# Attention plus FP4 feed-forward on one core: pairing two steps of the middle batches on TensorE

## The reference

```python
x = x + attention(layernorm(x), ctx, ctx)     # ctx: 1601 rows, 16 heads of 16 features
x = x + ffn(layernorm(x))

attn = softmax(einsum('bhqd,bhkd->bhqk', q, k) * scale)
out  = einsum('bhqk,bhkd->bhqd', attn, v)
h    = silu(fp4_linear(x, w_gate)) * fp4_linear(x, w_up)   # blocks of 16 rounded to FP4
y    = fp4_linear(h, w_down)
```

## Time and profile before

| what | value |
|---|---|
| timed runs | 1724.98 us median of 3 (1724.56 to 1728.42) |
| the profiled execution | 1726.32 us, span 1724.5 us |
| TensorE busy | 1653.4 us, 96% of the span |
| VectorE / ScalarE busy | 1427.4 us (83%) / 1132.4 us (66%) |
| mean granted TensorE clock | 0.991 |

### The profile page before, as it was taken

How to read it: one execution, slowest core, us unless ns; L and a number is a source line. 1 busy time by engine, 2 the same in 40 slices (tenths; PEclk the granted TensorE clock), 3 DMA queues, 4 the chain that set the end, 5 groups by cost and what they waited for, 6 DMA issues and landing times.

```text
span 1724.5 us, 27130 instructions
## 1 busy us (share of the span) xinstructions
PE 1653.4 (96%) x9496; PEld 666.1 (39%) x9496; DVE 1427.4 (83%) x2078; ACT 1132.4 (66%) x2295; POOL 553.3 (32%) x667
## 2 busy tenths in 40 slices
PE   6899899999999999999999999999999999989978
PEld 4332234333433344333443334333443334323345
DVE  5878988988798978898889887898879887898447
ACT  3377677766777667776677667776677766666731
POOL 5238520732025320443107321263303431013303
PEclk9899999999999999999999999999999999999989
DMA  6745332431235332142323323254222323200000
GB/s 166 158 81 136 70 70 45 97 98 36 57 59 118 74 63 55 49 116 48 78 45 77 105 43 60 45 120 86 52 53 60 81 48 67 44 8 10 13 22 13
DMA packets 106771, 117.53 MB, mean 68 GB/s; under 512 B 23236, under 2 KB 88140, under 8 KB 106636
## 3 DMA queue, kind: packets, MB, share of 16 engines
q1 hardware_dynamic: 101808, 111.62, 30.7%
q10 hardware_dynamic: 4828, 4.18, 1.0%
HBM read 76.78 MB, written 30.16 MB: 62 GB/s over the span
## 4 chain that ended last, share of the span: by engine, by line
PE 82%; DVE 11%; ACT 4%; issue 2%; DMA 1%; POOL 0%; ACTq 0%; SPq 0%; DVEq 0%
PE pvb L871 21%; PE st L837 20%; PE mx L856 10%; PE misc L758 7%; DVE cmx L1120 5%; PE misc L720 5%; PE misc L713 4%; PE misc L779 3%; ACT prob L1042 2%; PE misc L771 2%; PE misc L699 2%; PE misc L767 1%; PE misc L799 1%; PE misc L808 1%; DVE ht L1149 1%
## 5 line engine op out<-in xcount | busy, mean ns | idle before, releaser
L1042 ACT ACTIVATE prob<-st 128x512 f32<-128x512 f32 (+1 forms) x1591 | 867.6, 599 | 374.7 <-PE st L837 371.2
L1120 DVE TENSOR_REDUCE cmx<-mx 128x2 f32<-128x1024 f32 x768 | 904.9, 1219 | 150.5 <-PE mx L856 145.4
L837 PE MATMUL st<-qstack,kstack 112*128 112x512 bf16 (+1 forms) x1591 | 496.9, 384 | 8.5 <-ACT prob L1042 2.4
L871 PE MATMUL pvb<-prob,vv 128*32 128x512 f32 (+1 forms) x3328 | 444.2, 606 | 0.6 <-ACT prob L1042 0.6
L837 PEld LDWEIGHTS st<-qstack,kstack 112*128 112x128 bf16 (+1 forms) x1591 | 128.1, 98 | 463.4 <-issue 236.4
L856 PE MATMUL mx<-kstack,qstack 48*128 48x512 bf16 (+1 forms) x2048 | 256.8, 336 | 18.4 <-DVE cmx L1120 18.0
L1385 POOL TENSOR_TENSOR ht<-ht,rh 128x352 f32<-128x352 f32 (+1 forms) x78 | 56.9, 751 | 418.1 <-DVE rh L1096 418.1
L758 PE MATMUL misc<-wguT,rowsT 128*128 128x352 f32 x456 | 153.7, 458 | 0.0
L1377 POOL TENSOR_TENSOR ht<-ht,mt 128x352 f32<-128x352 f32 (+1 forms) x136 | 120.8, 911 | 69.5 <-DVE mt L1283 60.1
L856 PEld LDWEIGHTS mx<-kstack,qstack 48*128 48x128 bf16 x2048 | 59.8, 94 | 199.7 <-issue 138.0
L1391 POOL TENSOR_TENSOR cin<-cin 128x400 f32<-128x400 f32 (+1 forms) x60 | 55.7, 928 | 250.6 <-ACT cin L967 250.6
(11 more groups left out here) (192 smaller groups left out, 1558.5 us busy)
## 6 DMA issues: line engine op xcount, KB each, us to landing
kstack<-scr_k SPq DMA_DIRECT2D x378, 100.1 KB, 4.4
scr_k<-cin SPq DMA_DIRECT2D x48, 300.0 KB, 4.1
qstack<-scr_q SPq DMA_DIRECT2D x372, 32.0 KB, 1.9
cin<-ctx_in SPq DMA_DIRECT2D x16, 512.0 KB, 5.4
scr_q<-qp SPq DMA_DIRECT2D x16, 384.0 KB, 4.3
scr_k<-cin SPq DMA_DIRECT2D x16, 300.8 KB, 4.8
xn<-x SPq DMA_DIRECT2D x8, 512.0 KB, 3.9
cin<-ctx_in SPq DMA_DIRECT2D x16, 256.0 KB, 5.6
```

What stands on the lines that cost most here:

```text
L837: mm(score_bank(it, n, h)[0:KROWS[kt], :], kstack[:, hd, KOFF[kt]:KOFF[kt] + KROWS[kt]], qstack[:, hd, :], start=True, stop=True).then_inc ...
L871: last = mm(pvb[2 * D * h:2 * D * (h + 1), :], vv[0:w, kt, (HG * g + h) // 2, D * (h % 2):D * (h % 2 + 2)], prob[0:w, n % 2, h, :], start= ...
L1042: activate(prob[0:KROWS[kt], n % 2, 2 * pair + h, :], score_bank(it, n, 2 * pair + h)[0:KROWS[kt], :], ACT.Exp, scale=SCALE).then_inc(exp_ ...
L1120: v.tensor_reduce(cmx[:, g % 2, h0:h0 + 2, at:at + 1], products, op=ALU.max, axis=AX.X).then_inc(max_free, 1)
```

## The change

In "loop" iterations two steps are taken together, an even step n-1 and the odd step n. `maxima_with` puts no M in the even step; the odd step does M of n-1 after its scores and M of n at its end. `weighted_behind` (all batches with attention) puts both W into the odd step: those of n-2 and n-1. VectorE's extras of the even step follow the first M, those of the odd step the second. Since W comes later, `prob` has three buffers; room for it comes from `qp` (now in `ht`), `qx` (now in `x1` or `rowsT`) and `hqT` (now in `xa`), with three new waits that guard these places. Jobs that came at even steps from the side lists move to odd steps, and some down and gate jobs trade places.

```diff
-    10: ([("k", 1, "early")], [("nm", 1, "att")]),
-    11: ([("q", 0, "early")], []),
+    10: ([("k", 1, "early")], []),
+    11: ([("q", 0, "early")], [("nm", 1, "att")]),
...
+def weighted_behind(n):
+    if n in (1, 2 * NKT, 2 * NKT + 1):
+        return [n - 1]
+    return [n - 2, n - 1] if n % 2 and n > 1 else []
...
+def maxima_with(kind, n):
+    if kind != "loop":
+        return [n], []
+    return ([n - 1], [n]) if n % 2 else ([], [])
...
-        prob = sb("prob", [128, 2, HG, S])
+        prob = sb("prob", [128, 3, HG, S])
...
-                    products = maxima(it, n)
+                    products, behind = ([job for m in steps for job in maxima(it, m)] for steps in maxima_with(it.kind, n))
...
-                    if n and has_att:
-                        weighted(n - 1, "att")
-                    elif n == 0 and has_late:
+                    for m in weighted_behind(n) if has_att else []:
+                        weighted(m, "att")
+                    if n == 0 and has_late:
                         weighted(STEPS - 1, "late")
-                    for job in products[2:]:
+                    for job in products[2:] + behind:
                         pair_products(job)
...
-                        need(act, pv_done, it.count("att", STEPS, n - 1))
+                        need(act, pv_done, it.count("att", STEPS, n - 2))
...
-                    todo = maxima(it, n)
-                    for job in todo:
-                        maximum(job)
+                    before, behind = maxima_with(it.kind, n)
+                    for m in before:
+                        for job in maxima(it, m):
+                            maximum(job)
```

More of the change, by code:

```diff
@@ L94 @@
     20: ([("gate", 0, "late"), ("bob", 0, "once")], []),
-    21: ([("gate", 1, "late")], [("nm", 2, "att")]),
-    22: ([("up", 0, "late"), ("wT", 0, "once")], [("xqT", 1, "late")]),
-    23: ([("up", 1, "late"), ("wT", 1, "once")], []),
+    21: ([("gate", 1, "late")], []),
+    22: ([("up", 0, "late"), ("wT", 0, "once")], []),
+    23: ([("up", 1, "late"), ("wT", 1, "once")], [("nm", 2, "att")]),
     24: ([("gate", 2, "late")], []),
-    25: ([("gate", 3, "late"), ("wT", 2, "once")], []),
+    25: ([("gate", 3, "late"), ("wT", 2, "once")], [("xqT", 1, "late")]),
     26: ([("up", 2, "late"), ("wT", 3, "once")], []),
     27: ([("up", 3, "late")], [("hqT", 0, "late")]),
[L102 to L113, removed]
+    28: ([("gate", 4, "late")], []),
+    29: ([("gate", 5, "late")], [("hqT", 1, "late")]),
+    30: ([("down0", 0, "late")], []),
+    31: ([("down", 0, "late"), ("wT", 4, "once")], []),
+    32: ([("up", 4, "late"), ("wT", 5, "once")], []),
+    33: ([("up", 5, "late")], [("hqT", 2, "late")]),
+    34: ([("gate", 6, "late")], []),
+    35: ([("gate", 7, "late"), ("wT", 6, "once")], [("nm", 3, "att"), ("hqT", 3, "late")]),
+    36: ([("down0", 1, "late"), ("wT", 7, "once")], []),
+    37: ([("down", 1, "late")], [("hqT", 4, "late")]),
+    38: ([("up", 6, "late")], []),
+    39: ([("up", 7, "late")], [("hqT", 5, "late")]),
     40: ([("down0", 2, "late"), ("wT", 8, "once")], []),
@@ L117 @@
     43: ([("v", 1, "early")], [("hqT", 6, "late")]),
[L118 to L121, removed]
+    44: ([("v", 2, "early")], []),
+    45: ([("v", 3, "early")], [("hqT", 7, "late")]),
+    46: ([("down0", 3, "late"), ("wT", 10, "once")], []),
+    47: ([("down", 3, "late"), ("wT", 11, "once")], []),
     48: ([("v", 4, "early")], []),
-    49: ([("v", 5, "early")], []),
+    49: ([("v", 5, "early")], [("nm", 0, "early")]),
     50: ([("v", 6, "early")], []),
@@ L437, in score_bank, with queries_whole, probs @@
             return st[:, b, :] if b < 2 else misc[:, :] if b == 2 else mx[:, 0, b - 3, :]
+        def queries_whole(it):
+            return x1[:, 0:2, :].rearrange("p t n -> p (t n)") if it.kind in ("pre", "first") else rowsT[:, 1, :]
+        def probs(it, part, n):
+            return prob[:, (it.batch(part) * STEPS + n) % 3, :, :]
         def rows_rounding(it, k):
@@ L870, in weighted @@
                     for h in range(HG):
-                        last = mm(pvb[2 * D * h:2 * D * (h + 1), :], vv[0:w, kt, (HG * g + h) // 2, D * (h % 2):D * (h % 2 + 2)], prob[0:w, n % 2, h, :], start=(kt == 0), stop=(kt == NKT - 1))
+                        last = mm(pvb[2 * D * h:2 * D * (h + 1), :], vv[0:w, kt, (HG * g + h) // 2, D * (h % 2):D * (h % 2 + 2)], probs(it, part, n)[0:w, h, :], start=(kt == 0), stop=(kt == NKT - 1))
                     last.then_inc(pv_done, 1)
@@ L975, in take @@
                     elif kind == "xqT":
+                        if "early" in it.parts:
+                            act.wait_ge(q_split, it.count("early", 2, 2))
                         last = copy(rowsT[:, :, 256 * j:256 * (j + 1)], src.rearrange("p (c n) -> p c n", c=NC2))
@@ L1148, in take @@
                         dve.wait_ge(tanh_done, c(2 * QT, j + 1))
+                        if j == 4 and "early" in it.parts:
+                            dve.wait_ge(q_out, it.count("early", 32, 32))
                         v.scalar_tensor_tensor(ht[:, t, half * IH:(half + 1) * IH], th[j % 2], 1.0, src[:, 0:IH], op0=ALU.add, op1=ALU.mult).then_inc(free["gate"], 1)
@@ L1335, in body @@
                             weight_powers(W_POWER_AT[n])
-                    for part, what, k in EXTRAS[it.kind].get(n, []):
-                        if part in it.parts:
-                            extra(part, what, k)
+                    extras = [e for m in before for e in EXTRAS[it.kind].get(m, []) if e[0] in it.parts]
+                    for part, what, k in extras:
+                        extra(part, what, k)
+                    for m in behind:
+                        for job in maxima(it, m):
+                            maximum(job)
+                        for part, what, k in EXTRAS[it.kind].get(m, []):
+                            if part in it.parts:
+                                extra(part, what, k)
                 assert it.kind == "tail" or all(made[p] in (0, LINKS["late" if p == "late" else "early"]) for p in ("next", "early", "late")), made
@@ L1411, in work @@
                         pool.wait_ge(free["q"], c(2, k + 1))
-                        split(qx[:, :], qp, q_step, lambda n: c(4, 2 * k + n), q_split)
+                        split(queries_whole(it), qp, q_step, lambda n: c(4, 2 * k + n), q_split)
                     elif what == "k":
```

17 lines of the change are left out of this document (8 added, 9 removed).

## The result

The changed kernel takes 1987.36 us (median of 4 runs, 1981.94 to 1990.91) against 1726.52 us before: a ratio of 1.151, 95% interval 1.149 to 1.153. It is 15% slower, 8 us over the forecast of 1979.

The account below looks back on a forecast made before the run. TensorE sets the pace. A middle batch gains 29.0 + 4.3 + 6.6 + 3.0 + 3 - 5.5 = 40.4 us, six 242, plus 12 for first and last: 1979 us, 15% slower, range 1880 to 2065.

Parts of the forecast that it names:

- Switches: TensorE, paired M and W: fewer drains between matmul kinds save 0.23 us a pair, 5.5 us a middle batch.
- The score banks: S0' waits for S1's exponentials, starting e after S1 (ScalarE's remaining work for J): e + 0.49 a pair, 29.0 us a batch.
- I take it whole: The 29.0 us bank wait counts in full: J', S1', M, W and M' queue behind S0' on TensorE.
- M' behind the reductions: M' waits for VectorE's reductions of M: 0.25 us in 10 pairs, more in two special pairs; +4.3 a middle batch.
- Gates and output projection behind VectorE: Late VectorE work behind steps 23, 27, 33 and in 5, 7: +6.6 us a middle batch, bounds 0 and 10.
- Step 13: S0 of step 13 waits for maxima transfers, nm moved to step 11 behind four reductions: +2.7 us a middle batch.
- What I cost at nothing: Third prob buffer, new homes of qp, qx, hqT, and moved down jobs: no cost, guards wait for steps-old work.
- The clock: Long waits drop TensorE's clock: two or three stretches a batch at 1 to 1.5 us, +3, bounds 1 and 14.
- First and last: First and last batches, M between S1 and S0' hides 0.63 of the wait: about 9 us and 3 us.
- The sum: All terms: 40.4 us a middle batch, 242 for six, plus 12 for first and last, 254 together.

Follow-up runs that it names:

- other banks: Changed kernel with S0' of the odd step in two free banks of mx in the middle batches: 1919.80 us.
- the two edits: nm of the second group back at step 10 and hscale after the next evacuation, both added to the changed kernel with S0' in banks of mx: 1861.64 us.
- the old order: Changed kernel with M and W in every step again, keeping the new job table, third prob buffer, new places and guards: 1764.26 us.
- nm at 10: nm of the second group back at step 10, in two runs: M and W in every step with the new table, 1740.06 us; changed kernel, 1972.72 us.

## Why the prediction was right, point by point

**Switches, -0.23 us a pair: right where it can be seen.** Steps 40 and 41 with other banks show 0.25 (7.82 to 7.57). In other pairs of that run with the jobs of before it doesn't show, with waits left in them: steps 8 and 9 are 0.06 us longer than before, 16 and 17 0.40.

**The score banks, e + 0.49 a pair, 29.0 us a middle batch: right, in each term.** In a middle batch of the changed kernel the extra distance from S1 to the second matmul of S0', over 0.44 and 0.22, sums to 27.4 us over 23 pairs (27.3 by the forecast; 26.1 in the last of the six batches); the 24th, steps 12 and 13, lies under the transfers. By the job of the even step the extra is 1.65 us for k (forecast 1.66), 1.24 on the mean for v and xnT (1.27), 1.04 for gate (1.05) and 0.90 for up and down0 (0.90). The k pair above has each term.

**"I take it whole: nothing else can run meanwhile": right for adding.** The waits stand one behind the other in one order, and each adds to the sum. It doesn't follow that each can be taken away for its price, as the expectation for the other banks had it: with the banks given back only 68 us returned, not 6 x 29.0 = 174. The waits for VectorE that grew there, and the 58 us of the two edits instead of 15 + 27, fit that VectorE had been working off its queue during the wait for the banks.

**M' behind the reductions, +4.3 us a middle batch: a little high.** The single terms of the prediction add up to 4.2. It is 0.30 in the pair above, and over the 26 pairs of a middle batch the distance from M' to the next S0, over 0.55, sums to 3.1 to 3.4 us. Ten pairs with 0.25 were forecast; eight or nine have 0.1 to 0.3.

**Gates and output projection behind VectorE, 6.6 us: too high by a third.** Step 25 waits 1.71 us for the gate (2.0 forecast):

```profile
881.73 2.33 PE L783 MATMUL misc<-wguT,rowsT 128*128 128x352 f32 x4 [1.71 <-DVE ht L1180]
```

In the middle batches the gates' waits are 17.9 and the attention values' 10.1 us, 4.7 a batch in place of 6.6, without the clock behind them.

**Step 13, +2.7: right, its cause only half.** The timeline from S1 of step 12:

```profile
820.23 0.59 PE L862 MATMUL st<-qstack,kstack 112*65 112x512 bf16 x2
824.66 1.04 PE L862 MATMUL st<-qstack,kstack 112*128 112x512 bf16 x2 [3.83 <-DMA qstack<-nmp]
825.49 2.53 PE L738 MATMUL misc<-ctxT,wk 128*128 128x400 f32 x4
```

S0' comes 4.43 us after S1 instead of the 1.82 that the banks alone ask for, 2.6 more. But I put it down to the split behind four reductions. In the old order, with two reductions, the same job at step 11 still cost 24 us in all, as the run with nm at 10 shows: the step that it moved by is enough.

**What I cost at nothing (the third buffer, the new homes, the moved down jobs): right; what I put down to the pairs' order was in part the table's.** Buffers and homes alone take 1726.45 us against 1726.62, and the steps with the moved down jobs 0.1 us a batch. But alone, in the old order, the table costs 38 us, mainly by nm at step 11 and, less, by nm and hscale behind step 23. The prediction had charged both places, step 13 and step 25, but as effects of the pairs (both behind four reductions). So the total came out with a cause that was half right. My expectation for the old order, that the table costs nothing, contradicted these two terms and missed by 29 to 44 us.

**The clock, +3 us a batch: the mechanism and the number of stretches right, the size rather low.** Two windows in steps 12 and 13 show it, the columns as in the earlier trace rows:

```profile
820.66:824.06 3.40, 0.17 (x1) 0.00 (x0) 2.59 (x9) 1.81 (x4) 2.31 (x3) 1.00 0.01 2
824.08:827.48 3.40, 2.82 (x5) 1.48 (x6) 0.00 (x0) 1.09 (x2) 0.36 (x1) 0.51 0.75 250
```

TensorE waits in the first at full clock, and works in the second at half; the k projection there takes 2.36 us to the next start (825.49 to 827.85 in the trace), 1.35 elsewhere. The middle batches have 15 such stretches, 2.5 a batch, at steps 5, 12 and 25, as many as forecast; two of them are twice as long. What one costs differs with the comparison. With 34.1 us of half clock taken away by dummy matmuls the span fell by 16.7: 0.49 us for each, 1.7 for a stretch of 3.4, where I had 1 to 1.5. The two batches of the run with nm at 10 give 0.39, or 1.3 for a stretch. And the four executions of the changed kernel fall in two: 1983 us at a mean granted clock of 0.974, 1991 at 0.966, 8 us for some 32 more at half, 0.24 for each. At 0.39 to 0.49 the 58.0 us are 3.8 to 4.7 us a batch.

**First and last, 9 and 3 us: low.** From first score to first score the first batch went from 195.9 to 207.8, and the last from 173.6 to 180.0 up to its last step. The table was not in those estimates: with nm at 10 the first batch of the changed kernel takes 202.5, and in the old order the new table alone brings the last to 176.0. Each also has 3 to 4 us more at half clock.

**The sum.** Forecast 242 for six middle batches; measured 6 x (241.7 - 202.2) = 237. First and last 18 instead of 12. The banks, three quarters of it, were right to within 1 us a batch; that the rest meets the forecast so closely is partly luck, because the terms of VectorE were some 3 us a batch too high and the clock, the first and the last batch too low.

## What to carry to other kernels

Work that stands between two uses of a buffer may be its cover. Before regrouping instructions to save switches, count for each double buffer what the distance between its uses was, and what will stand there after: here 0.23 us saved in switches cost 0.9 to 1.65 us of waiting for two banks. Waits in one order add up when they are put in, but do not come back one by one when they are taken out: look at which wait ends next. A table of slots is part of the order; move a job one step later only after following its result to the one that waits for it.

## What the runs showed of the hardware that I had not expected

A long wait can be paid twice. In step 12 TensorE waits at full clock, and the next 3.4 us run at 1.2 GHz in place of 2.4. Filling such waits with matmuls that nobody reads took 34.1 us of half clock away and gave 16.7 us back, although the kernel still waits elsewhere.

Shortening one wait can move the fall to another place: with nm at 10 the time at half clock in the middle batches rose from 58.0 to 71.7 us, with stretches at steps 19 and 35 that the changed kernel has not, and with the other banks for S0' to 64.8, although both kernels were faster.

The same operation on VectorE, 16x128 with f32 in and out, took 0.28 us beside an idle POOL and 1.26 where POOL was at work on 128x512 for most of that time.
